# Decoder layer on one core: compact stacking rows, a two-term softmax shift sent from GpSimd, and a re-spaced step table

## The reference

```python
x = x + self_attention(layernorm(x), ...)          # softmax(q k^T / 4), causal
x = x + cross_attention(layernorm(x), ctx, mask)   # softmax(q k^T / 4), masked keys
x = x + mixture(layernorm(x), ...)                 # gate softmax, top 512 tokens per expert
```

## Time and profile before

| | us |
|---|---|
| median of 3 executions | 1594.34 (1589.86 to 1600.79) |
| the profiled execution | 1589.86 |
| its span, first to last instruction | 1588.1 |
| turn 3 (steps "st" 192 to 255) | 300.3 to 369.3 |
| turn 4 | 369.3 to 433.3 |
| turn 12 | 932.5 to 1011.5 |
| attention, first "p1" to last "st" | 78 to 1227 |

### The profile page before, as it was taken

One profiled execution on the slowest core, in us unless ns is written; L12 is line 12 of the kernel. 1 busy time (PEld: TensorE's weight loads), 2 busy tenths in 40 slices (PEclk: granted clock), 3 DMA queues, 4 the chain that ended last, 5 costly groups with the idle time before them and its releaser, 6 DMA issues. The chain is left out here.

```text
span 1588.1 us, 22489 instructions
## 1 busy us (share of the span) xinstructions
PE 1290.2 (81%) x7628; PEld 741.0 (47%) x7628; DVE 1095.4 (69%) x2822; ACT 643.3 (41%) x1288; POOL 556.5 (35%) x727
## 2 busy tenths in 40 slices
PE   6478888888888888888999889898888303988985
PEld 5344545444454444434444434343333302877874
DVE  5277777677776778878677777777772485778783
ACT  1014444344443444555454554545564000433431
POOL 4563443625436442222222131311101111455553
PEclk9669889798997999999999998999996655999998
DMA  4421423314133342342414141313101310343422
GB/s 142 93 63 46 94 64 84 73 48 94 50 86 87 94 102 66 83 103 70 88 61 94 54 94 54 80 41 81 41 2 40 130 34 14 94 133 84 122 61 28
DMA packets 90409, 117.96 MB, mean 74 GB/s; under 512 B 13057, under 2 KB 60161, under 8 KB 90178
## 3 DMA queue, kind: packets, MB, share of 16 engines
q1 hardware_dynamic: 84162, 108.12, 26.9%
q0 software_dynamic: 6144, 8.52, 3.2%
HBM read 48.76 MB, written 16.91 MB: 41 GB/s over the span
## 5 line engine op out<-in xcount | busy, mean ns | idle before, releaser
L685 ACT ACTIVATE probs<-ps_st 128x512 f32<-128x512 f32 (+3 forms) x1024 | 477.0, 516 | 479.6 <-PE ps_st L567 460.5
L567 PE MATMUL ps_st<-qst,kst 64*128 64x512 f32 (+3 forms) x1024 | 401.9, 443 | 103.5 <-ACT probs L685 102.9
L585 PE MATMUL ps_p<-kst,qst 63*128 63x512 f32 (+3 forms) x1024 | 409.0, 453 | 15.1 <-DMA kst<-qk_h 8.3
L567 PEld LDWEIGHTS ps_st<-qst,kst 64*128 64x128 f32 x1024 | 179.1, 196 | 443.6 <-ACT probs L685 272.3
L751 DVE TENSOR_REDUCE mx<-ps_p 128x1 f32<-128x512 f32 x512 | 327.2, 682 | 55.6 <-PE ps_p L585 54.6
L753 DVE CUSTOM_DVE_ANT_0 ps_p<-ps_p,tri 128x128 f32<-128x128 f32 (+3 forms) x512 | 241.7, 511 | 56.9 <-PE ps_p L585 54.0
L553 PE MATMUL ps_o<-probs,vals 128*32 128x512 f32 (+3 forms) x2048 | 250.7, 565 | 0.0
L585 PEld LDWEIGHTS ps_p<-kst,qst 63*128 63x128 f32 x1024 | 179.2, 197 | 44.5 <-issue 12.1
L459 POOL TENSOR_SCALAR_AFFINE_SELECT probs<-probs 128x512 f32<-128x512 f32 x128 | 79.6, 635 | 175.6 <-ACT probs L685 175.4
L406 POOL TENSOR_SCALAR lnw<-mv 128x4 f32<-128x4 f32 x24 | 4.7, 198 | 321.7 <-DVE mv L741 321.6
L1097 PE MATMUL moe_ps_y<-moe_w,moe_hid_h 128*128 128x256 f32 x512 | 98.7, 291 | 9.7 <-DVE moe_hid_l L1283 9.6
(11 more groups left out here) (189 smaller groups left out, 1978.3 us busy)
## 6 DMA issues: line engine op xcount, KB each, us to landing
qst<-qk_h SPq DMA_DIRECT2D x64, 256.0 KB, 4.4
kst<-qk_h SPq DMA_DIRECT2D x64, 256.0 KB, 5.7
qst<-qk_l SPq DMA_DIRECT2D x32, 256.0 KB, 5.1
kst<-qk_l SPq DMA_DIRECT2D x32, 256.0 KB, 5.2
moe_w1r<-in_w_dram SPq DMA_DIRECT2D x8, 1024.0 KB
moe_w2r<-in_w_dram SPq DMA_DIRECT2D x8, 1024.0 KB
xin<-in_x_dram SPq DMA_DIRECT2D x8, 512.0 KB, 5.2
xres<-in_x_dram SPq DMA_DIRECT2D x8, 512.0 KB, 3.9
```

The costliest lines, as they stand in the source:

```text
L567: last = nc.tensor.matmul(out, kst[rows, t % 2, pair, kt * P:(kt + 1) * P], qst[rows, t % 2, pair, lo:S], start=True, stop=not masked)
L585: last = nc.tensor.matmul(ps_p1[:, i % 3, 0:keys], qst[rows, t % 2, pair, qt * P:(qt + 1) * P], kst[rows, t % 2, pair, 0:keys], start=True ...
L685: nc.scalar.activation(probs[:, kt, j, 0:n], ps_st[:, i % 2, 0:n], ACT.Exp, scale=float(DH) ** -0.5).then_inc(exp_done, 1)
```

## The change

- The rows of a head are put together: term 0 at partitions 0 to 15, term 1 at 16 to 31, term 2 at 32 to 47, the key mask at 48, the shift at 49 and 50. "p1" uses 49 partitions, "st" 51. kst starts as ones; its mask rows are set to zero by a DMA.
- The shift has two rows: "neg" makes the negated maxima in float32r and, in a second DVE instruction that waits for the first, what that rounding left. The transpose gives 32 rows instead of 16.
- The shift DMAs are issued by POOL, in its share of "mt", and no longer by SP. "mt" stands at step -10 (and, by the order of the put calls, ahead of "p1" of that step); there is no "shift" piece.
- Most pieces of a turn are put at other steps; "lg" is cut into two pieces with a bank each.

```diff
-KEY_ROW = 3
-SHIFT_ROW = 63
-P1_ROWS = 63
-ST_ROWS = 64
+TERMS = 3 * DH
+KEY_ROW = TERMS
+SHIFT_ROW = TERMS + 1
+P1_ROWS = TERMS + 1
+ST_ROWS = TERMS + 3
...
-        put(16 * g - 9, "mt", g)
-        put(16 * g - 7, "shift", g)
+        put(16 * g + 1 - AHEAD, "mt", g)
...
-        put(far + 23, "xt", t, 0)
-        put(far + 27, "xt", t, 1)
+        put(far + 20, "xt", t, 0)
+        put(far + 22, "xt", t, 1)
         for i in range(4):
-            put(far + (47, 51, 59, 67)[i], "qk", t, i // 2, i % 2)
-            put(far + (65, 67, 71, 76)[i], "stack", t, i // 2, i % 2)
-        put(near + 11, "v", t, 0)
-        put(near + 15, "v", t, 1)
+            put(far + 50 + 6 * i, "qk", t, i // 2, i % 2)
+            put(far + 55 + 6 * i, "stack", t, i // 2, i % 2)
+        put(near + 14, "v", t, 0)
+        put(near + 17, "v", t, 1)
...
-            put(after + 43, "xt3", t, 0)
-            put(after + 43, "xt3", t, 1)
-            put(after + 47, "lg", t)
+            put(after + 39, "xt3", t, 0)
+            put(after + 41, "xt3", t, 1)
+            put(after + 43, "lg", t, 0)
+            put(after + 45, "lg", t, 1)
...
-                        rows = slice(64 * r + term, 64 * r + 64, 4)
-                        sp.dma_start(dst[rows, t % 2, :, :].bitcast(F32),
+                        row = 64 * r + term * DH
+                        sp.dma_start(dst[row:row + DH, t % 2, :, :].bitcast(F32),
                                      part[:, side, r, :].bitcast(F32)).then_inc(stacked, 16)
...
+                    elif kind == "mt":
+                        g = s[1]
+                        pool.wait_ge(m_free, M[s] + 1)
+                        for r in range(2):
+                            row = 64 * r + SHIFT_ROW
+                            nc.gpsimd.dma_start(qst[row:row + 2, g // GROUPS % 2, g % GROUPS * 2:g % GROUPS * 2 + 2, :].bitcast(F32),
+                                                shift[16 * r:16 * r + 16, :].bitcast(F32)).then_inc(shifted, 16)
...
-                        last = nc.tensor.transpose(bank[0:16, 0:P], neg[:, :].bitcast(F32), ident[:, :])
+                        last = nc.tensor.transpose(bank[0:32, 0:P], neg[:, :].bitcast(F32), ident[:, :])
...
-                        nc.vector.tensor_scalar(out=neg[:, :], in0=mx[:, g % 2, :], scalar1=-1.0, scalar2=None,
-                                                op0=ALU.mult).then_inc(neg_ready, 1)
+                        part = neg[:, :].rearrange("p (r h n) -> p r h n", r=2, h=2)
+                        src = mx[:, g % 2, :].rearrange("p (r n) -> p r n", r=2)
+                        link(nc.vector.tensor_scalar(out=part[:, :, 0, :], in0=src, scalar1=-1.0, scalar2=None, op0=ALU.mult))
+                        nc.vector.scalar_tensor_tensor(out=part[:, :, 1, :], in0=src, scalar=-1.0, in1=part[:, :, 0, :].bitcast(F32),
+                                                       op0=ALU.mult, op1=ALU.subtract).then_inc(neg_ready, 1)
```

More of the change, by code:

```diff
@@ L162, in attention @@
         mx = sb("mx", [P, 2, 16], F32)
-        neg = sb("neg", [P, 16], F32R)
-        shift = sb("shift", [16, P], F32R)
+        neg = sb("neg", [P, 32], F32R)
+        shift = sb("shift", [32, P], F32R)
         oraw = sb("oraw", [P, S], F32)
@@ L301, in _ @@
                          dram["wc"].rearrange("(a p) c -> p a c", p=P)).then_inc(wc_loaded, 16)
-            sp.wait_ge(kst_zero, 1)
-            sp.wait_ge(qst_ones, 1)
+            sp.wait_ge(kst_ones, 1)
+            sp.wait_ge(zero_row, 1)
             for r in range(2):
-                row = 64 * r + SHIFT_ROW
-                sp.dma_start(kst[row:row + 1, :, :, :].bitcast(F32), qst[row:row + 1, :, :, :].bitcast(F32)).then_inc(ones_row, 16)
+                row = 64 * r + KEY_ROW
+                sp.dma_start(kst[row:row + 1, :, :, :].rearrange("p a b s -> p (a b) s").bitcast(F32),
+                             zeros.unsqueeze(1).to_broadcast([1, 2 * PAIRS, S])).then_inc(key_row, 16)
             sp.dma_start(bqk[:, :, :], dram["b_qk"]).then_inc(small_loaded, 16)
@@ L330, in _ @@
                     for term, part in enumerate(((qk_h, qk_h, qk_l), (qk_h, qk_l, qk_h))[side]):
-                        rows = slice(64 * r + term, 64 * r + 64, 4)
-                        sp.dma_start(dst[rows, t % 2, :, :].bitcast(F32),
+                        row = 64 * r + term * DH
+                        sp.dma_start(dst[row:row + DH, t % 2, :, :].bitcast(F32),
                                      part[:, side, r, :].bitcast(F32)).then_inc(stacked, 16)
-                elif kind == "shift":
-                    g = s[1]
-                    sp.wait_ge(m_free, M[("mt", g)] + 1)
-                    for r in range(2):
-                        row = 64 * r + SHIFT_ROW
-                        sp.dma_start(qst[row:row + 1, g // GROUPS % 2, g % GROUPS * 2:g % GROUPS * 2 + 2, :].bitcast(F32),
-                                     shift[8 * r:8 * r + 8, :].bitcast(F32)).then_inc(shifted, 16)
                 elif kind == "resload":
@@ L344, in _ @@
                         sp.wait_ge(stored, 16 * t)
+                    else:
+                        sp.wait_ge(key_row, 32)
                     if t > B:
@@ L602, in run @@
                         pe.wait_ge(m_free, M[("xt3", t, 1)] + 1)
-                        for i in range(TT):
-                            at = slice(i * P, (i + 1) * P)
+                        for i in range(2):
+                            at = slice((2 * s[2] + i) * P, (2 * s[2] + i + 1) * P)
                             for k in range(KT):
@@ L800, in run @@
                     elif kind == "lg":
-                        at = (s[1] - B) * TT
-                        nc.vector.tensor_tensor(out=logits[:, at:at + TT, :], in0=bank[:, 0:TT * E_N].rearrange("p (t e) -> p t e", e=E_N),
-                                                in1=rb[:, :].unsqueeze(1).to_broadcast([P, TT, E_N]), op=ALU.add).then_inc(m_free, 1)
+                        at = (s[1] - B) * TT + 2 * s[2]
+                        nc.vector.tensor_tensor(out=logits[:, at:at + 2, :], in0=bank[:, 0:2 * E_N].rearrange("p (t e) -> p t e", e=E_N),
+                                                in1=rb[:, :].unsqueeze(1).to_broadcast([P, 2, E_N]), op=ALU.add).then_inc(m_free, 1)
                     elif kind == "mt":
@@ L806, in run @@
                             dve.wait_ge(shifted, 32 * s[1])
-                        nc.vector.tensor_copy(shift[:, :], bank[0:16, 0:P]).then_inc(m_free, 1)
+                        nc.vector.tensor_copy(shift[:, :], bank[0:32, 0:P]).then_inc(m_free, 1)
                     elif kind == "og":
```

33 lines of the change are left out of this document (17 added, 16 removed).

## The result

The median of the kernel after is 1763.97 us (1743.29 to 1774.1, 4 executions), of the kernel before on the same chip 1592.1 (4 executions): 172 us more. The ratio of the two is 1.099, with a 95% interval of 1.087 to 1.112, which is 158 ± 19 us of 1590. 1640 was forecast, and the range ended at 1698. The profiled execution took 1745.73 us, its span is 1744.0.

A forecast was written before the change was run, and what follows sets the result against it. PE was taken to bound the attention, at a pace set by its clock. Terms 27 + 20 + 2 - 10 - 8 + 5 + 10 = +46 us gave 1636, forecast as 1640 by the median; range 1586 to 1698.

The forecast's parts named there:

- The stacking DMAs ... I take 2, between 0 and 4.: Stacking DMAs at a turn's start: even at half rate they end under cover; +2 us, for the kernel's start.
- Landing takes 1.7 us ... up to 5.7. I take 3.: Shift DMAs: time to land after POOL's issue, 1.7 to 5.7 us, taken as 3.
- In cross turns it is busy 19 of 79 us; there the cover of ten steps holds and I count nothing.: POOL in cross turns: early enough with the shift DMAs, so no stall and no cost counted.
- The shift DMAs on POOL, 27 us.: Second group of turns 0 to 6: POOL issues the shift late, PE stalls; +27 us, bounds 7 to 52.
- "mt" earlier, "neg" in two, 20 us.: PE's wait for "neg" at "mt" grows in 64 groups; +20 us, between 0 and 58.
- The table, -10, -8 and +5.: New steps: "qk" spacing -10 us, gate cut in two -8, "ot" and "xt" closer +5.
- the rival "faster": Slow-clock stretches behind double "qk" and gate go altogether; about -38 us, 1556; chance 0.12.
- Moving the other pieces costs nothing, since PE's sum stays: Remaining pieces put at other steps: no cost, since PE's total work is unchanged.
- Fewer partitions in use perhaps lowering the clock too (nothing in the rows shows that): Possible addition in the rival with late shift and clock at their bounds, about 1695 us; chance 0.15.
- The clock, +10.: Stalls in seven turns may lower the granted clock; +10 us, between 0 and 28.
- The rival "the stacking becomes the bound": At a third of the rate stacking outlasts its cover in 14 turns; +126 us, 1740 or more; chance 0.05.
- No such wait in cross turns: Sign in the profile after: PE's "st" waits for the shift DMA only in turns 0 to 6, not cross turns.

The follow-up runs named there:

- before_newtable: The kernel before with only the step table of the kernel after, SP still issuing the shift; 1531.5 us, ratio 0.962 to the kernel before.
- nt_close64: before_newtable with a head's rows side by side, but the shift still at 63 and 63 and 64 rows used; 1634.9 us, ratio 1.029 to the kernel before.
- nt_pool: before_newtable with the shift DMAs issued by POOL instead of SP; 1571.1 us, ratio 0.989 to the kernel before.
- after_sp: The kernel after with the shift DMAs issued by SP instead of POOL, at the same step; 1706.1 us, ratio 1.077 to the kernel before.
- nt_neg2: before_newtable with "neg" in two DVE instructions and a 32-row transpose and copy, only the first term sent; 1568.1 us, ratio 0.988 to the kernel before.
- after_oldtable: The kernel after with the step table of the kernel before, "lg" still in two pieces; 1778.2 us, ratio 1.118 to the kernel before.
- before_step3: The kernel before with a term's partitions 3 apart in 0 to 47 and 49 and 50 rows used; 1637.2 us, ratio 1.031 to the kernel before.
- before_close: The kernel before with a head's rows side by side, 49 and 50 rows used, SP's issue and old table; 1707.5 us, ratio 1.075 to the kernel before.
- nt_close: before_newtable with a head's rows side by side and 49 and 50 rows used; 1698.7 us, ratio 1.069 to the kernel before.

## Why the prediction was wrong, point by point

I forecast +46 us; it was +158 by the ratio, +172 by the medians. The account on top of the new table, each part alone: table -60, neg +41, POOL +42, stacking at half the rate +105, number of rows +64 (with the slow stacking in place), together +192. That is 34 over the whole, with some 10 to 16 us of noise in each term. The parts may overlap as well: "neg" and POOL's issue cost 14 ± 14 and 35 ± 22 with the slow stacking in place.

- **"The stacking DMAs ... I take 2, between 0 and 4."** This is the step that failed: the term measured 105 ± 16 us (before_newtable to nt_close64). The halved rate was expected, and the trace agrees with it (213 to 121 GB/s; the Trainium skill, SBUF — State Buffer, "Door 1: The DMA port swizzle", had 196 to 104). I asked whether the stacking DMAs are in time for the work that reads them, and they are: "p1" waits for one of them once, 12.2 us. I did not ask who else is in the DMA engines meanwhile. The shift of the second group is, and it comes out among the last of them.
- **"Landing takes 1.7 us ... up to 5.7. I take 3."** Right for stacking at the old rate: in nt_pool it is 3.4. Behind stacking at half the rate it is 8 to 14. I used the landing time of before for a queue that I had just doubled.
- **"In cross turns it is busy 19 of 79 us; there the cover of ten steps holds and I count nothing."** POOL is early there, as said: in turn 12 it issues at R + 9.5. PE wants the shift at R + 16.8 (1106.61 less 7.02), and gets it at R + 23.8. The cover of ten steps was sized by POOL's work, and the transfer outlasts it.
- **The shift DMAs on POOL, 27 us.** The mechanism and its place are shown by nt_pool, turns 0 to 7 (one more than I had) and 2.8 to 6.9 us each, 30.0 us of waits. Its price is 42 ± 14 alone and 35 ± 22 on top of the slow stacking (after_sp to after): I gave the stalls, and too little for the clock behind them. The stalls of turns 0 to 6 in the kernel after, 4.6 to 11.0 us, pass my upper bound of 7.4, which left out a landing of 5.7 that I had named myself; with 3.9 it is 15.1 + 3.3 + 3.9 - 14.7 = 7.6. An issue took 0.585 us in the mean, less than the 0.71 that I had as the lower bound.
- **"mt" earlier, "neg" in two, 20 us.** 41 ± 15 alone. The rise of the wait by 21 us and its 48 times were right ("about 40 us and 50 times"; nt_neg2 has 35.5 and 48, the kernel after 26.2 and 45); its price in time is more than the waits. Under the close rows it costs 14 ± 14; that PE waits for the shift there anyway may be why, no run tests it.
- **The table, -10, -8 and +5.** It is -60 ± 11. What I had as the rival "faster", the slow stretches behind "qk" and the gate going altogether (-20, -27 and -8, together -55), is what the table alone does, with the sign it gave for it: the clock of a cross turn is 1.00. Put back by themselves, the gate's steps cost 26 ± 19 and those of qk and stack 18 ± 19. "Moving the other pieces costs nothing, since PE's sum stays" was wrong too: PE's waits for ACT fell from 102.9 to 70.0 us. That pieces which stood in a heap now stand beside steps that go at ACT's pace is my reading of it; the two runs that put steps back restore 13.5 of these 33 us. In the kernel after the gain is smaller (30 ± 22 us, after_oldtable), where the clock is low for another reason.
- **The number of rows.** "Fewer partitions in use perhaps lowering the clock too (nothing in the rows shows that)" stood in a rival at 0.15, without a price. It costs 34, 67, 36 and 64 us in four pairs that differ by it alone (before_step3, before_close, after, nt_close), and the sum had nothing for it: the second step that failed.
- **The clock, +10.** It fell from 0.888 to 0.816. PE's busy time alone grew by 81 us. My price, 4 us of a turn for 0.10 of clock, came from a stretch that began 2.6 us into turn 3; the whole turn lasts 69.0 us and not 66.4, which makes it 5.
- **The rival "the stacking becomes the bound", 1740 or more, at 0.05.** Its time is the nearest of all, by luck. It had the next turn's "p1" waiting for the stacking in 14 turns, and "p1" waits once. What half the rate delays is the shift.

Of what was to show it: waits of "st" in turns 0 to 6 came, and stacking later than 5.7 us, and "neg" 45 times, and DVE's wait for POOL's qk_l fell from 29.5 to 19.1 us. "No such wait in cross turns" was wrong, and that one line, seven waits of 4.9 to 7.3 us, says that the cause was not POOL alone.

## What to carry to other kernels

When a transfer gets slower, look not only at who reads it, but at every small transfer that is issued while it runs: with the DMA engines full, a DMA of 8 KB took up to 14 us here, as long as the DMAs of 256 KB issued beside it, from whichever queue it came. Fewer partitions in a matmul save nothing here and may cost clock; take the rows that are free, filled so that they add nothing. And a heap of small pieces in a static order is worth spreading: at the same sum of work it gave 3.8%.

## What the runs showed that I had not expected

- Matmuls over 49 and 50 partitions instead of 63 and 64, with the same instructions and columns and about the same waits, made the kernel 34 to 67 us slower by the granted clock (0.856 against 0.887, 0.812 against 0.877). Which property of the rows it is, their number or what they hold, is open: the added rows hold 1 in one operand and 0 in the other, and no run had other values there.
- Terms 3 partitions apart over 48 are in between: kst<-qk_h lands after 10.1 to 11.2 us, against 4.5 to 6.8 for 4 apart over 64 and 13.6 to 14.1 side by side.
- A shift DMA on SP's queue behind nine stacking DMAs and one on POOL's own queue come equally late: 13.8 us from issue to PE's start in nt_close64 (833.48 to 847.32), 14.3 in after.

```profile
833.48 1.44 SPq L340 DMA_DIRECT2D qst<-shift  x2
```

```profile
847.32 0.79 PE L568 MATMUL ps_st<-qst,kst 64*128 64x512 f32 x1 [4.66 <-DMA qst<-shift]
```
